# Decoder layer: in the last attention batch, heads turned by groups for all rows, three quarters of the out product taken ahead, LayerNorm roots in pairs

## The chip, the cores and the metric

The kernel runs on one core of one Trainium2 chip. The metric is the device time of one execution in microseconds (us). An execution was profiled once; instruction times below are us from the start of its span. PE is TensorE, PEld its weight loads, DVE is VectorE, ACT ScalarE, POOL GpSimd, SP SyncE, which here only issues DMAs.

## What is computed

```
x = layernorm(x + attention(x, Wq, Wk, Wv, Wo))      # x: (4, 512, 512), 16 heads of 32
x = layernorm(x + experts(x, token ids, ctx))        # 4 experts of 512x512, one per row
x = layernorm(x + ffn(x, w_gate, w_up, w_down))      # 2:4 sparsified hidden layer of 2048
```

Attention: `scores = q k^T`, masked by multiplication with a lower triangle (so masked scores are 0 and still take part), softmax of `scores / sqrt(512)`, times v, heads side by side, times Wo. LayerNorm has no weights: `(x - mean) / sqrt(var + 1e-5)`. In the expert stage each token goes through the expert that its token id chooses, `silu(x W) * (x W)` times W with W from ctx, and is added to x.

## The kernel before

**Stages.** `attention` is one block of instructions for all five engines, `late` (experts and FFN) the next. At the end of a block all engines meet at a barrier and jump; the first instructions of `late` stand behind it. `late` begins with SP loading 128-row tiles of `sorted_dram` (L1424), the DRAM buffer into which attention's rows are scattered in the order of their experts, and with PE turning the first of them (L1513). PE then runs almost without a gap to the end.

**Precision.** Products are made of three: a number is kept as a high part (`_hi`, rounded by an ACT copy) and a low part (`_lo`, the DVE difference), and `matmul3` (L32) issues hi*hi, hi*lo and lo*hi for each of the four slices of 128 of the contraction: 12 matmuls of 128x512 for a 128x512 output tile.

**Attention.** A batch has 512 rows in four row blocks r of 128 and 16 heads in four groups m of 4 heads (128 columns of the concatenated heads). A head has three units u: row blocks (2, 0), then 3, then 1, so a batch has 48 units. For a unit, PE makes scores (L462), DVE their maxima (L764, L775, L778), ACT the exponentials `probs` (L619), PE transposes them (L473), ACT and DVE halve them (`pt_hi` L629, `pt_lo` L784), PE multiplies with v (L489, two units later), and after a head's third unit ACT copies its output out of PSUM (`copy_out`, L654) and POOL adds its parts (L227 to L230). When a group of 4 heads is there, `norm_heads` divides it by the softmax sums into `o_raw`: on POOL for m = 0, 1, 2 (six instructions, about 6.6 us), on DVE for m = 3, where nothing follows it. The order on each engine is written out by hand: `batch(b, more)` in the block of each engine; `more` is false in the last batch (b = 3).

**The end of a batch**, in the order of the list `between`: for each row block r, PE turns all 4 groups of `o_raw` (`turn_heads`, L528: 4 transposes of 128x128 into one bank, one for each group), ACT and DVE halve the turned block (`turned_hi` L663, `turned_lo` L816), PE takes the out product with Wo (`out_product`, 12 matmuls), DVE adds x (`add_x`, L828) and takes mean and variance (`ln.statistics`, L938 and L940), POOL makes 1/sqrt(var + eps) (`ln.rstd`, L969, L973), and the row block is normalized. In the first three batches this is done by ACT with a bias `-mean/sqrt` that POOL makes too (L971, L977; `scale_act` L964), in the last batch by DVE (`ln.scale`, L945). POOL then issues the indirect DMA that scatters the 128 rows (L352). POOL works in order: root of r, then the DMA of r - 1. After the last DMA it waits until all scatters have landed (`pool.wait_ge(s_sc, ...)`) before it goes to the barrier.

In the last batch ACT and DVE also cut the expert weights into high and low parts at the end: `cut_hi` (L1237) for experts 0 to 3 and `cut_lo` (L1241) for experts 0 and 1 before the adds; `cut_lo` for 2 and 3 is DVE's first work in `late`.

## Time and profile before

| | us |
|---|---|
| median of 3 runs | 1136.07 |
| lowest and highest run | 1134.1, 1136.53 |
| the profiled execution | 1132.93 |
| its span (first to last instruction) | 1131.1 |
| PE busy | 1045.4 (92%) |
| DVE busy | 746.5 (66%) |
| ACT busy | 480.6 (42%) |
| POOL busy | 291.2 (26%) |

The attention block takes the first 446 us. Of the page's 40 equal slices of the span, PE is least busy, between 0.4 and 0.5, in the one from 424 to 452. A timeline row reads: start, duration, engine, line and operation, output from inputs, how many merged, and in brackets how long the engine had been idle before it and whose result ended that. `<-issue` means that nothing in the profile explains the wait.

### The profile page before, as it was taken

To read this page: it belongs to the slowest core of one execution; us is meant where nothing else is said; L and a number is where in the kernel's file an instruction comes from. 1 tells how busy PE (TensorE), PEld (TensorE's weight loads), DVE (VectorE), ACT (ScalarE), POOL (GpSimd) and SP (SyncE) were. 2 spreads that over 40 slices of the span, in tenths; PEclk is the share of its full clock that TensorE was granted. 3 is DMA by queue.
4 is the path that set the end of the run, shared out by engine and by line. 5 is a ranking of instruction groups with operands and counts; after the bars stand their busy time and mean duration, and the time that the engine had idled before them with its cause. 6 is when DMAs were issued, how large, how long until landed. Compare 5 with 4: busy or idle time off the path is not lost.

```text
span 1131.1 us, 18084 instructions
## 1 busy us (share of the span) xinstructions
PE 1045.4 (92%) x6022; PEld 845.0 (75%) x6023; DVE 746.5 (66%) x1765; ACT 480.6 (42%) x890; POOL 291.2 (26%) x490
## 2 busy tenths in 40 slices
PE   7889988999998864999999999999999999999994
PEld 6667776767776653788788888888888888888873
DVE  5898699768868886465756655555565545664666
ACT  5787488648846891222324213221232122221113
POOL 2186346544733642123220004100000000000222
PEclk9999999999999987999999999999999999999997
DMA  8877266726743742123533003310020001100101
GB/s 256 239 182 201 65 196 182 202 75 168 200 119 103 190 157 74 38 84 105 193 130 119 23 1 38 38 38 1 1 75 22 16 0 37 37 1 1 38 38 75
DMA packets 55217, 106.19 MB, mean 94 GB/s; under 512 B 6240, under 2 KB 8288, under 8 KB 55136
## 3 DMA queue, kind: packets, MB, share of 16 engines
q1 hardware_dynamic: 50256, 90.99, 29.0%
q0 software_dynamic: 4880, 14.18, 3.4%
q8 instruction: 44, 0.72, 0.3%
q14 instruction: 37, 0.30, 0.1%
HBM read 72.11 MB, written 30.94 MB: 91 GB/s over the span
## 4 chain that ended last, share of the span: by engine, by line
PE 56%; DVE 2%; DMA 1%; ACT 0%; issue 0%; POOLq 0%; POOL 0%; ACTq 0%; SPq 0%; DVEq 0%
PE f_bank L42 54%; PE f_bank L1521 1%; PE f_bank L1513 1%; PE f_bank L1563 1%; DVE rows_kept L1860 0%; DVE ln_stats L938 0%; DMA fw_raw<-gate 0%; DMA rows<-sorted_dram 0%; DVE hs_lo L1848 0%; DVE gu L1764 0%; DVE ln_mv L940 0%; ACT L951 0%; POOLq L1307 0%; DVE h L1838 0%; ACT hs_hi L1690 0%
## 5 line engine op out<-in xcount | busy, mean ns | idle before, releaser
L1667 ACT ACTIVATE fsg<-f_bank 128x512 f32<-128x512 f32 x64 | 38.3, 599 | 298.6 <-PE f_bank L42 298.5
L1799 DVE TENSOR_TENSOR h<-f_bank,fsg 128x512 f32<-128x512 f32 x64 | 44.2, 691 | 181.2 <-PE f_bank L42 181.1
L473 PE MATMUL bank<-ident,probs 128*128 128x128 f32 x640 | 108.8, 285 | 33.8 <-DVE pt_lo L784 22.7
L764 DVE CUSTOM_DVE_ANT_0 bank<-bank,mask 128x384 f32<-128x384 f32 (+3 forms) x256 | 123.1, 503 | 20.2 <-PE bank L462 19.6
L619 ACT ACTIVATE probs<-bank,nmax 128x384 f32<-128x384 f32 (+3 forms) x256 | 129.7, 539 | 15.0 <-DVE nmax L775 13.4
L969 POOL TENSOR_SCALAR ln_var<-ln_mv 128x1 f32<-128x1 f32 x43 | 10.0, 232 | 466.2 <-DVE ln_mv L940 464.9
L784 DVE TENSOR_TENSOR pt_lo<-bank,pt_hi 128x512 f16<-128x512 f32 (+1 forms) x192 | 114.7, 597 | 15.4 <-ACT pt_hi L629 15.0
L629 ACT ACTIVATE pt_hi<-bank 128x512 f16<-128x512 f32 (+1 forms) x192 | 103.0, 536 | 34.1 <-PE bank L473 33.4
L42 PE MATMUL bank<-x_hi,w_qk 128*128 128x512 f32 x256 | 104.3, 416 | 6.8 <-DVE x_lo L789 6.8
L42 PE MATMUL f_bank<-wd_hi,hs_hi 128*128 128x512 f32 x256 | 100.4, 392 | 3.2 <-DVE rows_kept L1860 3.2
L473 PEld LDWEIGHTS bank<-ident,probs 128*128 128x128 f32 x640 | 67.0, 141 | 45.4 <-ACT probs L619 22.4
L42 PE MATMUL f_bank<-wd_hi,hs_lo 128*128 128x512 f32 x256 | 100.4, 392 | 0.0
L42 PE MATMUL f_bank<-wd_lo,hs_hi 128*128 128x512 f32 x256 | 100.1, 391 | 0.0
L42 PE MATMUL f_bank<-big_hi,wg_hi 128*128 128x512 f32 x240 | 93.8, 391 | 0.0
L42 PE MATMUL f_bank<-big_hi,wu_lo 128*128 128x512 f32 x240 | 93.5, 389 | 0.0
L42 PE MATMUL f_bank<-big_hi,wg_lo 128*128 128x512 f32 x240 | 93.4, 389 | 0.0
L42 PE MATMUL f_bank<-big_lo,wg_hi 128*128 128x512 f32 x240 | 93.4, 389 | 0.0
L42 PE MATMUL f_bank<-big_hi,wu_hi 128*128 128x512 f32 x240 | 93.4, 389 | 0.0
L42 PE MATMUL f_bank<-big_lo,wu_hi 128*128 128x512 f32 x240 | 93.4, 389 | 0.0
L462 PE MATMUL bank<-big_lo 128*128 128x384 f32 (+3 forms) x256 | 83.2, 371 | 1.1 <-DMA big_lo<-k_lo_dram 1.1
L489 PEld LDWEIGHTS bank<-v,pt_hi 128*128 128x128 f16 x640 | 49.6, 97 | 39.4 <-issue 29.1
L489 PE MATMUL bank<-v,pt_hi 128*128 128x97 bf16 x640 | 75.0, 211 | 2.3 <-DVE pt_lo L784 2.1
(236 smaller groups left out, 2452.8 us busy)
## 6 DMA issues: line engine op xcount, KB each, us to landing
big_lo<-q_hi_dram SPq DMA_DIRECT2D x32, 256.0 KB, 4.0
big_lo<-q_lo_dram SPq DMA_DIRECT2D x32, 256.0 KB, 4.5
big_lo<-k_hi_dram SPq DMA_DIRECT2D x32, 256.0 KB, 3.9
big_lo<-k_lo_dram SPq DMA_DIRECT2D x32, 256.0 KB, 5.2
rows<-sorted_dram SPq DMA_DIRECT2D x19, 256.0 KB, 2.7
q_hi_dram<-q_hi SPq DMA_DIRECT2D x16, 256.0 KB, 2.4
q_lo_dram<-q_lo SPq DMA_DIRECT2D x16, 256.0 KB, 2.5
k_hi_dram<-k_hi SPq DMA_DIRECT2D x16, 256.0 KB, 3.5
```

The costliest lines, as they stand in the source:

```text
L42: ins = pe.matmul(out, a(k, i), b(k, j), start=(n == 0), stop=(n == len(chain) - 1))
L462: ins = pe.matmul(S[u % SR][:, at:at + cols(r)], stack[0][m % 2][:, h, r * P:(r + 1) * P], stack[1][m % 2][:, h, 0:cols(r)], start=True, s ...
L473: ins = pe.transpose(TP[u % TR][:, j * P:(j + 1) * P], probs[u % RP][:, j * P:(j + 1) * P], ident[:, :])
L489: ins = pe.matmul(out[:, at:ONE + 1], p, v3[:, j, c, at:ONE + 1], start=(n == 0), stop=(n == len(chain) - 1))
L619: ins = act.activation(probs[u % RP][:, at:at + cols(r)], S[u % SR][:, at:at + cols(r)], ACT.Exp, bias=nmax[:, r, c:c + 1])
L629: act.activation(pt_hi[u % RP][:, 0:n], TP[u % TR][:, 0:n], ACT.Copy).then_inc(s_hi, 1)
L764: dve.tensor_tensor_reduce(out=S[u % SR][:, at:at + cols(r)], in0=S[u % SR][:, at:at + cols(r)], in1=mask[:, T - cols(r):T], scale=1.0, sc ...
L784: dve.tensor_tensor(pt_lo[u % RP][:, 0:n], TP[u % TR][:, 0:n], pt_hi[u % RP][:, 0:n], ALU.subtract).then_inc(s_lo, 1)
L1513: ins = pe.transpose(XB[q % 2][:, k * P:(k + 1) * P], rows[q][:, k * P:(k + 1) * P], ident[:, :])
L1521: ins = pe.transpose(EG[i][:, k * P:(k + 1) * P], gu[i][:, k * P:(k + 1) * P], ident[:, :])
L1667: act.activation(fsg[v % 2][:, :], GB[v % 2][:, :], ACT.Silu).then_inc(s_sg, 1)
L1799: dve.tensor_tensor(h[r % 2][:, j, :], UB[v % 2][:, :], fsg[v % 2][:, :], ALU.mult).then_inc(s_h, 1)
```

## The change

The last batch gets its own end; the other three keep `between`.

- PE turns **groups for all rows**: `turn_group(m)` transposes group m of all four row blocks into one bank, behind units 25, 33 and 46 for m = 0, 1, 2 and behind the heads for m = 3. ACT and DVE halve each (`group_hi`, `group_lo`, 128x512) one unit later into slice m of `x_hi` and `x_lo`, which held x turned.
- PE takes the **out product in two parts**: `last_product(r, 0, 9)`, the nine matmuls of groups 0 to 2, at unit 48 for row block 0 (ahead of unit 46 times v), at unit 49 for row block 1 (ahead of unit 47 times v), behind that for 2 and 3; then group 3 is turned and halved and each row block gets its last three matmuls. The four outputs lie in four banks.
- DVE adds and takes statistics for all four row blocks; `cut_lo` of experts 0 and 1 stands behind these. ACT does its four `cut_hi` around `group_hi(3)` and then normalizes all row blocks.
- POOL makes the **roots in pairs** (four instructions on two columns each), then issues two DMAs, twice.
- The wait for the scatters moves from POOL's end of `attention` to SP's first load (and to POOL's start) in `late`, behind the barrier.

```diff
-                for n in range(NB + 1):
-                    if n < NB:
-                        ln.rstd(pool, b * NB + n, n, more)
...
-            pool.wait_ge(s_sc, B * NB * 16)
+                else:
+                    for n in range(0, NB, 2):
+                        ln.rstd(pool, b * NB + n, n, tiles=2)
+                        for r in (n, n + 1):
+                            place(r)
...
+            def turn_group(m):
...
+                for r in range(NB):
+                    ins = pe.transpose(turn_bank(m)[:, r * P:(r + 1) * P],
+                                       o_raw[:, r, m * HPT:(m + 1) * HPT, :].rearrange("p h d -> p (h d)"),
+                                       ident[:, :])
+            def last_product(r, first, last):
+
+                pe.wait_ge(s_otl, LAST * NB + (last + 2) // 3)
+                return matmul3(pe, LB[r][:, :], lambda k, i: x_hl[i][:, k, r * P:(r + 1) * P],
+                               lambda k, i: (wh, wl)[i][3][:, k, :], KT, first, last)
...
+                    if not more and u in part_at:
+                        last_product(part_at[u], 0, 3 * (KT - 1))
                     if u + AHEAD_V >= 0:
                         values(b, u + AHEAD_V)
+                    if not more and u in turn_at:
+                        turn_group(turn_at[u])
+                if not more:
+                    for r in range(len(part_at), NB):
+                        last_product(r, 0, 3 * (KT - 1))
+                    turn_group(NM - 1)
+                    for r in range(NB):
+                        last_product(r, 3 * (KT - 1), 3 * KT).then_inc(s_wo, 1)
...
+                if not more:
+                    group_lo(NM - 1)
+                    for r in range(NB):
+                        add_x(b, r)
+
+                    dve.wait_ge(s_vp, B * NB)
+                    for e in range(len(context.raw) // 2):
+                        context.cut_lo(dve, e)
...
+            sp.wait_ge(s_sc, NT * 16)
             for n in range(3):
                 load(n, n)
```

PE at the end of the last head, before (a last unit times v, then bank by bank the transposes and products; bank4 and bank7 take the out products of row blocks 0 and 1):

```order
L489 MATMUL bank6<-v3,pt_hi3 128x97
L489 MATMUL bank6<-v3,pt_lo3 128x65
L528 MATMUL bank5<-ident,o_raw 128x128 x4
L528 MATMUL bank6<-ident,o_raw 128x128 x4
L42 MATMUL bank4<-big_hi,ot_hi0 128x512 x2
L42 MATMUL bank4<-big_hi,ot_lo0 128x512
```

The same place now (bank0 and bank1 take row blocks 1 and 2):

```order
L42 MATMUL bank0<-big_hi,x_lo 128x512
L505 MATMUL bank6<-v3,pt_hi3 128x97
L505 MATMUL bank6<-v3,pt_lo3 128x65
L505 MATMUL bank6<-v3,pt_hi3 128x97
L505 MATMUL bank6<-v3,pt_lo3 128x65
L42 MATMUL bank1<-big_hi,x_hi 128x512 x2
L42 MATMUL bank1<-big_hi,x_lo 128x512
L42 MATMUL bank1<-big_hi,x_hi 128x512 x2
L42 MATMUL bank1<-big_hi,x_lo 128x512
L42 MATMUL bank1<-big_hi,x_hi 128x512 x2
L42 MATMUL bank1<-big_hi,x_lo 128x512
```

Nine matmuls for row block 1 now stand ahead of the last unit times v, and 18 more between it and the last group's transposes, which were the next thing before.

POOL's last instructions of the attention block, before (`z0` to `z3` are the row blocks):

```order
L969 TENSOR_SCALAR ln1_var<-ln1_mv 128x1
L973 TENSOR_TENSOR ln1_r<-ln1_var,ln1_half 128x1
L352 DMA sorted_dram<-z1,idx_all 2432x512
L969 TENSOR_SCALAR ln1_var<-ln1_mv 128x1
L973 TENSOR_TENSOR ln1_r<-ln1_var,ln1_half 128x1
L352 DMA sorted_dram<-z2,idx_all 2432x512
L352 DMA sorted_dram<-z3,idx_all 2432x512
```

and now:

```order
L357 DMA sorted_dram<-z0,idx_all 2432x512
L357 DMA sorted_dram<-z1,idx_all 2432x512
L1031 TENSOR_SCALAR ln1_var<-ln1_mv 128x2
L1033 TENSOR_SCALAR ln1_minus<-ln1_mv 128x2
L1036 TENSOR_TENSOR ln1_r<-ln1_var,ln1_half 128x2
L1040 TENSOR_TENSOR ln1_moved<-ln1_minus,ln1_r 128x2
L357 DMA sorted_dram<-z2,idx_all 2432x512
L357 DMA sorted_dram<-z3,idx_all 2432x512
```

The second pair's roots moved behind the DMAs of the first pair.

## Rows read from the trace of the kernel before

**Rows 1.** Stretches: start:end, length, busy of PE, PEld, DVE, ACT, POOL, clock, DMA.

```profile
404.00:408.00 4.00, 2.99 (x40) 2.49 (x36) 3.60 (x15) 3.77 (x10) 3.78 (x5) 1.00 0.86 314
...
416.00:428.00 12.00, 8.22 (x29) 6.44 (x29) 9.20 (x14) 8.88 (x7) 0.01 (x1) 0.58 0.00 1
...
437.00:450.00 13.00, 0.12 (x2) 0.05 (x1) 5.87 (x7) 0.00 (x0) 4.83 (x10) 0.69 0.33 116
```

**Rows 2.** The chain of waits that ended last, where the attention block ends.

```profile
446.62 3.29 DMA rows<-sorted_dram
```

**Rows 3.** Timeline of ACT: copies of heads 6 and 7, in batches 2 and 3.

```profile
280.98 0.49 ACT L654 ACTIVATE o_part<-bank 128x388 f32<-128x388 f32 x1
...
285.36 0.56 ACT L654 ACTIVATE o_part<-bank 128x388 f32<-128x388 f32 x1
...
383.46 0.49 ACT L654 ACTIVATE o_part<-bank 128x388 f32<-128x388 f32 x1
...
387.29 0.49 ACT L654 ACTIVATE o_part<-bank 128x388 f32<-128x388 f32 x1
```

**Rows 4.** Timeline of ACT and DVE around the end of the last head.

```profile
414.43 0.51 ACT L654 ACTIVATE o_part<-bank 128x388 f32<-128x388 f32 x1
...
416.27 0.49 ACT L654 ACTIVATE o_part<-bank 128x388 f32<-128x388 f32 x1 [0.77 <-PE bank L489]
...
414.58 0.69 DVE L784 TENSOR_TENSOR pt_lo<-bank,pt_hi 128x512 f16<-128x512 f32 x1 [0.16 <-ACT pt_hi L629]
```

**Rows 5.** Timeline of PE behind the heads.

```profile
419.45 1.94 PE L528 MATMUL bank<-ident,o_raw 128*128 128x128 f32 x8 [3.22 <-DVE o_raw L265]
421.95 1.22 PE L42 MATMUL bank<-big_hi,ot_hi 128*128 128x512 f32 x2 [0.56 <-DVE ot_lo L816]
...
427.24 1.05 PE L528 MATMUL bank<-ident,o_raw 128*128 128x128 f32 x4
...
434.83 0.63 PE L42 MATMUL bank<-big_hi,ot_hi 128*128 128x512 f32 x2
...
435.53 0.62 PE L42 MATMUL bank<-big_hi,ot_hi 128*128 128x512 f32 x2
```

**Rows 6.** Timeline of DVE: first add, what follows its statistics, last add and statistics.

```profile
427.48 0.69 DVE L828 TENSOR_TENSOR z<-bank,x_raw 128x512 f32<-128x512 f32 x1 [0.32 <-PE bank L42]
...
429.14 0.69 DVE L816 TENSOR_TENSOR ot_lo<-bank,ot_hi 128x512 fp32r<-128x512 f32 x1
...
437.11 0.69 DVE L828 TENSOR_TENSOR z<-bank,x_raw 128x512 f32<-128x512 f32 x1 [0.59 <-PE bank L42]
...
438.68 0.18 DVE L940 BATCH_NORM_AGGREGATE ln_mv<-ln_stats 128x2 f32<-128x6 f32 x1
```

**Rows 7.** Timelines of POOL and ACT: roots, normalizing and scatter, batches 3 and 2.

```profile
439.06 0.31 POOL L969 TENSOR_SCALAR ln_var<-ln_mv 128x1 f32<-128x1 f32 x1 [0.55 <-DVE ln_mv L940]
...
441.86 0.96 POOL L352 DMA_INDIRECT sorted_dram<-z,idx_all  x1 [0.31 <-issue]
...
342.24 0.23 POOL L969 TENSOR_SCALAR ln_var<-ln_mv 128x1 f32<-128x1 f32 x1 [4.04 <-DVE ln_mv L940]
...
343.45 0.19 POOL L977 TENSOR_TENSOR ln_moved<-ln_minus,ln_r 128x1 f32<-128x1 f32 x1
...
351.98 0.82 ACT L964 ACTIVATE z<-z,ln_moved,ln_r 128x512 f32<-128x512 f32 x1
...
353.62 0.96 POOL L352 DMA_INDIRECT sorted_dram<-z,idx_all  x1 [0.86 <-ACT z L964]
```

**Rows 8.** The scatter's line: the 16 DMAs' time to landing.

```profile
DMA to landing us min/median/max: 2.7/2.9/6.4
```

**Rows 9.** POOL's scatters in the late block, and DVE's cutting of expert weights.

```profile
577.39 1.07 POOL L1470 DMA_INDIRECT ordered_dram<-y,slot_idx  x1 [1.47 <-DVE y L945]
...
583.86 1.34 POOL L1470 DMA_INDIRECT ordered_dram<-y,slot_idx  x1 [1.47 <-DVE y L945]
...
422.67 4.48 DVE L1241 TENSOR_TENSOR big_hi<-rows_kept,big_lo 128x2048 fp32r<-128x2048 f32 x2
```

More of the change, by code:

```diff
@@ L213, in attention, with turn_bank @@
         rows_at = {1: 2, 3: 3}
+        LAST = B - 1
+        LB = (PJ, S[0], S[1], S[2])
+        turn_at = {25: 0, 33: 1, 46: 2}
+        part_at = {UPB: 0, UPB + 1: 1}
+        def turn_bank(m):
+            return PJ if m < NM - 1 else TP[0]
         wo_at = {5 + 2 * k: k for k in range(KT)}
@@ L564, in batch @@
                         project(b, *pieces[u])
+                    if not more and u in part_at:
+                        last_product(part_at[u], 0, 3 * (KT - 1))
                     if u + AHEAD_V >= 0:
                         values(b, u + AHEAD_V)
-                for step, r in between:
-                    if step == "v" and more:
+                    if not more and u in turn_at:
[6 more added lines that the diff above has]
+                        last_product(r, 3 * (KT - 1), 3 * KT).then_inc(s_wo, 1)
+                for step, r in between if more else ():
+                    if step == "v":
                         v_product(r)
@@ L574, in batch @@
                         out_product(b, r)
-                    elif step == "scores" and more:
+                    elif step == "scores":
                         pe.wait_ge(s_vr, (b + 2) * NB)
@@ L579, in batch @@
                             scores(b + 1, u)
-                    elif step == "sum" and more:
+                    elif step == "sum":
                         v_sum(b + 1, r)
@@ L700, in batch @@
                         copy_out(b, u // UPH - 1)
+                    if not more and u - 1 in turn_at:
+                        group_hi(turn_at[u - 1])
                 above(b, NM - 1)
@@ L709, in batch @@
                         context.cut_hi(act, e)
-                for step, r in between:
-                    if step == "v" and more:
+                    group_hi(NM - 1)
+                    for e in range(2, len(context.raw)):
+                        context.cut_hi(act, e)
+                    for r in range(NB):
+                        norm_rows(b, r)
+                for step, r in between if more else ():
+                    if step == "v":
                         v_split(b + 1, (r, r + 1))
@@ L714, in batch @@
                         turned_hi(b, r)
-                        if not more and r == 1:
-                            for e in range(2, len(context.raw)):
-                                context.cut_hi(act, e)
-                    elif step == "scores" and more:
+                    elif step == "scores":
                         for u in range(AHEAD_S):
                             exps(b + 1, u)
-                    elif step == "out" and more and r >= 2:
+                    elif step == "out" and r >= 2:
                         norm_rows(b, r - 2)
@@ L852, in batch @@
                             v_above(0, n)
+                    if not more and u - 1 in turn_at:
+                        group_lo(turn_at[u - 1])
                 norm_heads(dve, 1, b, NM - 1)
-                for step, r in between:
-                    if step == "v" and more:
+                if not more:
+                    group_lo(NM - 1)
+                    for r in range(NB):
+                        add_x(b, r)
+                    dve.wait_ge(s_vp, B * NB)
+                    for e in range(len(context.raw) // 2):
+                        context.cut_lo(dve, e)
+                for step, r in between if more else ():
+                    if step == "v":
                         v_split(b + 1, (r, r + 1))
@@ L858, in batch @@
                         turned_lo(b, r)
-                        if not more and r == 1:
-                            dve.wait_ge(s_vp, B * NB)
-                            for e in range(len(context.raw) // 2):
-                                context.cut_lo(dve, e)
                     elif step == "out":
                         add_x(b, r)
-                        if r >= 1 and not more:
-                            norm_rows(b, r - 1)
-                    elif step == "scores" and more:
+                    elif step == "scores":
                         for u in range(AHEAD_S):
@@ L873, in batch @@
                         negated(b + 1, AHEAD_S - 1)
-                    elif step == "sum" and more:
+                    elif step == "sum":
                         v_above(b + 1, r)
-                if not more:
-                    norm_rows(b, NB - 1)
             def qk_lo(i):
@@ L1482, in _ @@
             for n in range(NS):
-                ln2.rstd(pool, n, n % 4)
+                ln2.rstd(pool, n, n % 4, False)
                 place(n)
```

72 lines of the change are left out of this document (48 added, 24 removed).

## Prediction

> **What bounds the kernel now.** I read the stretches first, then the timelines between us 404 and 450. In the heads all engines are close to full: of 4 us ACT works 3.77 and DVE 3.60, PE only 2.99 [rows 1]; a step added there for ACT or DVE is not free. Behind the heads PE waits 3.22 us for the last group's normalizing, then starts its transposes at 419.45, and between 416 and 428 has a mean clock of 0.58, most of it the lower level, 1.2 GHz [rows 1, 5]. From 421.95 to 427.24 it makes 12 matmuls, 0.44 us each; near 435 three take 0.70 us, 0.23 each [rows 5]. From 437 to 450 PE does nothing: the chain runs through DVE and POOL (adds, roots, scatters), the barrier, and the first load, issued at 446.62 and landed 3.29 us later [rows 1, 2]. Behind that load PE is full to the end, so the issue time of this load is what the change can move: each us there is a us of the kernel. The last scatter begins at 441.86, 4.76 us earlier [rows 7]. So the sum is: where does the last scatter begin now, and how long from it to the load.
>
> **1. Group turns in the heads.** Groups 0 and 1 add, at two places, 4 transposes on PE, one ACT copy and one DVE difference of 128x512 (0.69, as L784 in [rows 4]). PE has a quarter of its time idle; ACT and DVE have not. The nearest rows: in batch 2 the stretch from one head's copy to the next holds two more ACT copies (halving x) and takes 4.38 us (280.98 to 285.36), the same stretch of batch 3 without them 3.83 (383.46 to 387.29) [rows 3]: 0.28 for each. Here DVE's part comes on top, and for group 1 ACT also waits for PE's transposes. Bounds: 0.1 each, if the slack takes them, and 1.1 each, if both parts lie on the path. I take **+1.0** for both. POOL's norms of the groups end before the turns, so they add no wait.
>
> **2. Group 2 and the first partial products.** Group 2's turn stands behind unit 46's transposes; ACT halves it behind the copy of head 14, which starts at 414.43 [rows 4] and holds ACT 0.5, so to about 415.5; DVE's difference ends at 416.2. PE waits for it at unit 48, about 1 us, and then makes nine matmuls (2.1 us at 0.233), unit 46 times v (0.3), nine more (2.1), unit 47 times v. The copy of head 15, at 416.27 before [rows 4], starts at about 421.2: +4.9. Its copy and normalizing take 3.2 us as before (416.27 to 419.45) [rows 4, 5], to 424.4; PE meanwhile makes 18 matmuls (4.2 us) and is done at 425.25, so PE ends last, not DVE. The 3.22 us wait is gone.
>
> **3. The last group and the last quarter.** Transposes 0.6, ACT 0.6, DVE 0.7, three matmuls 0.9: the first add starts at 428.1. Before it was at 427.48 [rows 6]: **+0.7**, and with part 1 +1.7, so 429.1. The nine twelfths taken ahead save less than they cost here, because they stand ahead of the last head's own output. ACT's cut_hi still fit ahead of and behind the last group.
>
> **4. Adds.** From an add to the next instruction behind its statistics DVE takes 1.66 us (427.48 to 429.14), from the last add to the end of its variance 1.75 (437.11 to 438.86) [rows 6]. PE brings a row block every 0.7 us, so DVE sets the pace: first add to last variance 3*1.66 + 1.75 = 6.7 us instead of 11.4. **-4.7**: this is the gain of the change.
>
> **5. Roots and scatters.** Before, the last variance leads to the last scatter in 441.86 - 438.86 = 3.0 us [rows 6, 7]. Now count from the second variance, at 1.66 + 1.75 = 3.4 us behind the first add. POOL starts 0.2 later [rows 7]. The four root instructions take 1.4 us for one column (342.24 to 343.64); two columns and the slower 0.31 of L969 in batch 3 make it 1.66. ACT's normalizing takes 0.82, and the scatter that waits for it starts 0.82 after it ends (352.80 to 353.62) [rows 7]. A scatter lasts 0.96 to 1.1 and the next comes 0.31 later [rows 7], or lasts 1.34 beside DVE's cutting of weights [rows 9]: 1.4 between two, 1.07 for the second. Then the same again for the pair 2 and 3, whose variances are long there: POOL is the bound. 3.4 + 0.2 + 2*(1.66 + 0.82 + 0.82 + 1.4) + 1.07 + 0.2 = 14.3 us from first add to last scatter, plus 0.5 for scatters beside cut_lo, which now runs there: 14.8. Before it was 441.86 - 427.48 = 14.4. So the gain of part 4 is given back whole: **+5.1**, and parts 4 and 5 together are +0.4. The first pair costs two waits for ACT that DVE's scaling hid before.
>
> **6. The barrier.** Before: scatter at 441.86, landed 2.7 us later [rows 8] at 444.56, load issued at 446.62: 2.06 for POOL's waking, barrier and jump. Now POOL goes to the barrier when its last scatter's 0.96 is over, while it flies; barrier end is 0.96 + 0.2 + 1.9 = 3.06 behind its start, by when it has landed, and SP's new wait costs nothing. 3.06 instead of 4.76: **-1.7**. Bounds: 0, if the jump waits for something else than the engines, and -2.06. Queued behind SP's wait are only the loads that need it; DVE's two cut_lo (4.5 us) start with the barrier's end as before, and still end before ACT's first copy of the turned rows.
>
> **Sum.** +1.0 + 0.7 - 4.7 + 5.1 - 1.7 = **+0.4 us**; I say +0.5. The profiled execution had a span of 1131.1 and 1132.93 in all, 3.1 below the median 1136.07; the difference is carried over to the median: **1136.6 us**. A change of 0.2%, 2.3 us, is about what a measurement of this kernel can tell.
>
> **Rivals.**
>
> *A, a faster one: the heads take the turns into their slack, and POOL's and ACT's hand-overs are shorter.* The 0.82 from a finished ACT to the scatter is issue time; if it runs beside the root or beside the previous scatter, as in the two scatters 0.31 apart [rows 7], 2*0.5 is saved; +1.0 in the heads becomes +0.2; the clock level behind the barrier comes back up to a us sooner. -0.8 - 1.0 - 1 against +0.5: -2.3 and beyond, 1133.5. Against it: three scatters that waited for ACT all started that late.
>
> *B, DVE and POOL on one path to memory.* cut_lo, two instructions of 2.24 us each [rows 9], stood ahead of the adds, where POOL was idle; it now starts at the last variance, 6.7 us behind the first add, and ends 4.5 later, at 11.2. The second pair's roots start at 3.4 + 0.2 + 1.66 + 1.64 + 1.4 + 1.07 + 0.2 = 9.6. If POOL's small instructions must wait for the one that runs, they start at 11.2: +1.6, so +2.1 in all, 1138.2. Rows speak for little: beside four differences of 128x512 with both inputs in SBUF a scatter lasted 1.34 instead of 1.07 [rows 9]; but that is a scatter, and none shows a root in that place. The Trainium skill (SBUF — State Buffer, Who interferes with whom) says that a VectorE instruction with two SBUF inputs and a GpSimd instruction that reads SBUF exclude each other for the whole instruction, whoever is first. By that rule B is what happens.
>
> *C, slower: the clock.* PE stopped behind the heads and the granted clock was at the lower level for the transposes and the next 12 matmuls [rows 5]. In the new order PE stands about 1 us ahead of the nine matmuls of unit 48. If the clock falls there, the 36 matmuls ahead of the last group run at up to 0.43: 0.2 more each, 7 us, or, if it returns after the 7.8 us that it took before (419.45 to 427.24), 7.8/2 = 3.9; all of it is on the path. +0.5 + 3.5: 1140. It decides only if the stop at unit 48 is as long as the one before, 3.2 us; 1 us speaks against it.
>
> *D*: the wait in SP's queue or the jump keeps the whole 4.76: +2.2, 1138.3.
>
> **Chances.** Forecast 0.42, by itself 1135 to 1138.3. A 0.22, B 0.20, C 0.08, D 0.08. Range 1132.5 to 1140. Faster by over 0.2% (below 1133.8): A, 0.22. Slower by over 0.2% (above 1138.3): C, half of B and D, and the upper edge of the forecast: 0.25. Within: 0.53.
>
> **What would show it.** First add about 1.7 us later than 427.48, last variance near 436, last scatter near 443.9, first load near 447. Part 1: head copies behind us 387 later by 0.3 to 0.6 at units 26 and 34. Part 2: the copy of head 15 at about 422, PE busy without a gap over 1.5 us from there. B: POOL's first root of the second pair begins when a cut_lo ends. C: 0.4 us a matmul in the partial products. Wrong if the last scatter starts before 441 or the load is not 3 us behind it.

## The result

The changed kernel takes **1138.23 us** (median of 13 runs, 1136.32 to 1139.96); the kernel before took 1135.38 in the same series (13 runs, 1132.71 to 1136.53). The ratio is 1.0029, 95% interval 1.0020 to 1.0038: 0.29% slower. A second series, shown below, gave 1.0016 (1.0004 to 1.0028). The forecast was 1136.6 and "within 0.2%": the time lies inside the range, 1.6 us above the forecast. In us it stays just below the slow bound of 1138.3; as a ratio it is beyond 0.2% in this series and not in the second. It is rival B's number, 1138.2, and nearly rival B's mechanism, but the number is in part luck: B had +2.1 on 1136.07, and it was +2.85 on 1135.38.

### The profile after

The profiled execution has a span of 1136.0 us, 4.9 more than before. 1.70 of that arise ahead of everything that was changed: the copy of head 7 in batch 3 starts at 388.99, not at 387.29 [rows 3]. I therefore compare distances from that copy on, and from one landmark to the next.

ACT, timeline: the copies of heads 14 and 15 out of PSUM (answers to [rows 4]), and the two pairs of row blocks that it normalizes.

```profile
416.80 0.51 ACT L703 ACTIVATE o_part<-bank 128x388 f32<-128x388 f32 x1
423.61 0.50 ACT L703 ACTIVATE o_part<-bank 128x388 f32<-128x388 f32 x1 [5.44 <-PE bank L505]
...
435.96 1.52 ACT L1023 ACTIVATE z<-z,ln_moved,ln_r 128x512 f32<-128x512 f32 x2 [3.44 <-POOL ln_moved L1040]
444.48 1.52 ACT L1023 ACTIVATE z<-z,ln_moved,ln_r 128x512 f32<-128x512 f32 x2 [7.00 <-POOL ln_moved L1040]
```

PE, timeline: start of the partial products, the turn of the last group, and the last quarter (answers to [rows 5]).

```profile
418.57 0.73 PE L42 MATMUL bank<-big_hi,x_hi 128*128 128x512 f32 x2 [0.93 <-DVE x_lo L879]
...
427.69 0.60 PE L573 MATMUL bank<-ident,o_raw 128*128 128x128 f32 x4
429.70 0.73 PE L42 MATMUL bank<-big_hi,x_hi 128*128 128x512 f32 x2 [1.41 <-DVE x_lo L879]
```

DVE, timeline: first add, last variance, `cut_lo` (answers to [rows 6]).

```profile
430.70 0.69 DVE L890 TENSOR_TENSOR z<-bank,x_raw 128x512 f32<-128x512 f32 x1 [1.05 <-PE bank L42]
...
437.35 0.18 DVE L999 BATCH_NORM_AGGREGATE ln_mv<-ln_stats 128x2 f32<-128x6 f32 x1
437.45 4.49 DVE L1304 TENSOR_TENSOR big_hi<-rows_kept,big_lo 128x2048 fp32r<-128x2048 f32 x2
```

POOL, timeline: roots of a pair and two scatters, twice (answers to [rows 7]), and SP's first loads behind the barrier (to [rows 2]).

```profile
434.34 0.24 POOL L1031 TENSOR_SCALAR ln_var<-ln_mv 128x2 f32<-128x2 f32 x1 [15.95 <-DVE ln_mv L999]
...
437.60 3.12 POOL L357 DMA_INDIRECT sorted_dram<-z,idx_all  x1 [1.67 <-ACT z L1023]
441.03 1.76 POOL L357 DMA_INDIRECT sorted_dram<-z,idx_all  x1 [0.30 <-issue]
442.86 0.23 POOL L1031 TENSOR_SCALAR ln_var<-ln_mv 128x2 f32<-128x2 f32 x1
...
446.11 1.07 POOL L357 DMA_INDIRECT sorted_dram<-z,idx_all  x1 [1.67 <-ACT z L1023]
447.49 0.96 POOL L357 DMA_INDIRECT sorted_dram<-z,idx_all  x1 [0.31 <-issue]
...
451.56 0.13 POOL L992 MEMSET ln_half<- 128x1 f32 x2 [3.11 <-POOLq L69]
```

```profile
451.25 2.60 SPq L1487 DMA_DIRECT2D rows<-sorted_dram  x4
```

PE, timeline: the first turn of sorted rows in `late` and the fifth, before and after. By the fifth turn PE is back in its rhythm of one turn in about 6.45 us, so that is where I stop counting.

```profile
449.95 1.11 PE L1513 MATMUL f_bank<-ident,rows 128*128 128x128 f32 x4 [12.88 <-DMA rows<-sorted_dram]
...
475.61 0.60 PE L1513 MATMUL f_bank<-ident,rows 128*128 128x128 f32 x4
```

```profile
454.37 1.12 PE L1578 MATMUL f_bank<-ident,rows 128*128 128x128 f32 x4 [21.62 <-DMA rows<-sorted_dram]
...
480.48 0.60 PE L1578 MATMUL f_bank<-ident,rows 128*128 128x128 f32 x4
```

What to see: the first two scatter rows are the surprise. A scatter took 0.96 to 1.34 us in every row of before; here two take 3.12 and 1.76, and both begin inside DVE's `cut_lo` (437.45 to 441.94). The sum, step by step:

| from ... to | before | after | difference | predicted |
|---|---|---|---|---|
| copy of head 7 to copy of head 14 | 27.14 | 27.81 | +0.67 | +1.0 |
| to the first add | 13.05 | 13.90 | +0.85 | +0.7 |
| to the end of the last variance | 11.38 | 6.83 | -4.55 | -4.7 |
| to the last scatter | 3.00 | 9.96 | +6.96 | +5.1 |
| to the first load | 4.76 | 3.76 | -1.00 | -1.7 |
| to PE's first turn | 3.33 | 3.12 | -0.21 | 0 |
| to PE's fifth turn | 25.66 | 26.11 | +0.45 | 0 |
| sum | 88.32 | 91.49 | **+3.17** | +0.4 |

The 3.17 us agree with the 2.85 between the medians. But the column "before" is one execution, and a long one behind the heads: in e3 and h1 below, in which nothing is changed up to the last product, the first add came 12.64 us behind the copy of head 14 (13.05 here) and the last variance 10.54 and 10.78 behind the first add (11.38 here). In this profile the third row block's transposes still ran at the lower clock (1.05 us, [rows 5]; 0.60 in h1). Against those two the changed kernel's gain from the adds would be 3.7 to 4.0 and not 4.55.

### The profile page after: what moved, and what is told of

It reads as the page before. It is cut to its first block, busy times and chain, and to the rows that moved or that the text cites. A ratio compares the mean times of both kernels' runs of the same rounds, so it can differ in the third digit from the quotient of the medians.

```text
span 1136.0 us, 18082 instructions
## 1 busy us (share of the span) xinstructions
PE 1043.8 (92%) x6022; PEld 843.0 (74%) x6023; DVE 743.7 (65%) x1761; ACT 482.6 (42%) x894; POOL 293.9 (26%) x490
## 4 chain that ended last, share of the span: by engine, by line
PE 56%; DVE 2%; DMA 1%; ACT 0%; issue 0%; POOLq 0%; POOL 0%; ACTq 0%; SPq 0%; DVEq 0%
PE f_bank L42 54%; PE f_bank L1586 1%; PE f_bank L1578 1%; PE f_bank L1628 1%; DVE rows_kept L1925 0%; DVE ln_stats L997 0%; DMA fw_raw<-gate 0%; DMA rows<-sorted_dram 0%; DVE hs_lo L1913 0%; DVE gu L1829 0%; DVE ln_mv L999 0%; ACT L1010 0%; POOLq L1370 0%; DVE h L1903 0%; ACT hs_hi L1755 0%
## 5 line engine op out<-in xcount | busy, mean ns | idle before, releaser
L1031 POOL TENSOR_SCALAR ln_var<-ln_mv 128x1 f32<-128x1 f32 (+1 forms) x41 | 9.3, 228 | 463.5 <-DVE ln_mv L999 462.1
L489 PEld LDWEIGHTS bank<-ident,probs 128*128 128x128 f32 x640 | 67.5, 141 | 45.1 <-ACT probs L668 22.5
```

Of the source, the lines that this page charges most:

```text
L489: ins = pe.transpose(TP[u % TR][:, j * P:(j + 1) * P], probs[u % RP][:, j * P:(j + 1) * P], ident[:, :])
```

## The experiments

Theory P: `cut_lo` beside the scatters is what makes the change slow, by holding the scatters. Its rival O: the order of pairs itself (two waits for ACT, 1.67 us of idle each) is the price, and not the scatters' length. Every ratio below is to the kernel before on the same chip. Chips differ: the median of before was between 1133.75 and 1136.16 in the five series.

### cut_lo early: `e1_cut_early`

```diff
+                if not more:
+                    dve.wait_ge(s_vp, B * NB)
+                    for e in range(len(context.raw) // 2):
+                        context.cut_lo(dve, e)
                 norm_heads(dve, 1, b, NM - 1)
...
                     for r in range(NB):
                         add_x(b, r)
-
-                    dve.wait_ge(s_vp, B * NB)
-                    for e in range(len(context.raw) // 2):
-                        context.cut_lo(dve, e)
```

ACT's first two `cut_hi` move ahead of the copy of head 15 too.

> The change with one thing moved: the first two cut_hi of ACT and the two cut_lo of DVE stand in the wait for the last head's output instead of at the last group and behind the adds. Theory P (DVE's cut_lo, which reads two SBUF inputs, holds POOL up while it issues the scatters): with DVE free the first scatter takes 1.1 us instead of 3.12 and the second 0.96 to 1.1 instead of 1.76, so the second pair's roots start 2.7 us sooner, and from first add to last scatter it takes 14.1 us instead of 16.8; the time is 2.5 to 3 us under the change's, level with the kernel before. Rival Q (the first scatter is long for a reason of its own, it is the first work of POOL after a long idle stretch and its rows come from ACT): 3.1 and 1.8 us stay, and 16.8 us too. Both: PE's partial products are not later, since DVE has 4.7 us and ACT 5.4 us idle there.

Measured: 1133.13 us, ratio 0.9995 (0.9981 to 1.0009). POOL's timeline:

```profile
435.16 1.10 POOL L357 DMA_INDIRECT sorted_dram<-z,idx_all  x1 [1.67 <-ACT z L1023]
436.57 0.96 POOL L357 DMA_INDIRECT sorted_dram<-z,idx_all  x1 [0.30 <-issue]
437.60 0.23 POOL L1031 TENSOR_SCALAR ln_var<-ln_mv 128x2 f32<-128x2 f32 x1
```

The first pair's scatters take 2.06 us together, not 4.88, and from first add to last scatter it is 13.95 us in place of 16.79: the 2.84 are the scatters' 2.82. The copy of head 15 is as far behind that of head 14 as in the changed kernel (6.83 and 6.81), and the first add 0.21 later behind it (14.11 and 13.90), so `cut_lo` and `cut_hi` cost little in their new place. P holds, and within what these runs can tell (0.14% either way) its price is the whole loss against before.

### Single roots: `e2_single_roots` and `e4_early_single`

```diff
-                    for n in range(0, NB, 2):
-                        ln.rstd(pool, b * NB + n, n, tiles=2)
-                        for r in (n, n + 1):
-                            place(r)
+                    for n in range(NB + 1):
+                        if n < NB:
+                            ln.rstd(pool, b * NB + n, n, False)
+                        if n > 0:
+                            place(n - 1)
...
                         add_x(b, r)
+                        if r > 0:
+                            ln.scale(dve, z[r - 1], z[r - 1], b * NB + r - 1, r - 1, s_x1)
+                    ln.scale(dve, z[NB - 1], z[NB - 1], b * NB + NB - 1, NB - 1, s_x1)
```

This is the root, scaling and scatter order of the kernel before, behind the new adds; ACT no longer normalizes. e2 leaves `cut_lo` late, e4 moves it as e1 does.

> The change with the pairs undone: POOL makes one root at a time and scatters the row block before, as in the kernel before, and DVE normalizes; cut_lo stays behind DVE's last work. If the pairs with ACT's normalizing cost what the prediction said, two hand-overs from ACT of 0.82 + 0.82 us each and four root instructions instead of two, and the cutting the rest, then first add to last scatter falls from 16.8 us to 12 to 12.5 us: DVE takes 2.2 us for each row block with its scaling, last scaling near 9.5 us behind the first add, scatters about 2.6 us apart, and only the last one beside cut_lo. The time is then about 4 us under the change's, 1 us under the kernel before. Rival: POOL's issue of scatters alone is the bound (4 times 1.4 us behind each other): then single roots gain under 1 us.

> Both of the first two edits on the change: cut_lo early and single roots with DVE's scaling. If the two costs add up: first add to last scatter 12 us instead of 16.8 (14.4 in the kernel before), last scatter near 442.5 instead of 447.5 on the change's scale, and the time 4.5 to 5 us under the change's, 1.5 to 2 us under the kernel before. If cutting and pairs are one cost counted twice, it is no faster than the better of the two.

Measured: e2 1134.27 us, ratio 1.0002 (0.9991 to 1.0014); e4 1132.08 us, ratio 0.9981 (0.9972 to 0.9991), faster than both kernels. From first add to last scatter both take 10.89 us, less than the 12 to 12.5 expected (pairs with early `cut_lo`: 13.95). So the pairs have a price of their own beside P's, 3.06 us in the profiles. In the time e4 leads e1 by 0.14%, 1.6 us, with intervals that overlap; in the profiles 0.50 of the 3.06 go to the load's landing and 1.50 to the distance from first to fifth turn, 28.24 and 26.74. In e2 only the last scatter meets `cut_lo`. DVE and POOL there:

```profile
439.23 0.55 DVE L1006 TENSOR_SCALAR z<-z,ln_mv,ln_r 128x512 f32<-128x512 f32 x1 [0.77 <-POOL ln_r L1038]
439.69 4.49 DVE L1306 TENSOR_TENSOR big_hi<-rows_kept,big_lo 128x2048 fp32r<-128x2048 f32 x2
```

```profile
439.39 1.34 POOL L357 DMA_INDIRECT sorted_dram<-z,idx_all  x1 [0.19 <-issue]
441.03 1.78 POOL L357 DMA_INDIRECT sorted_dram<-z,idx_all  x1 [0.30 <-issue]
```

But e2's first load comes 4.58 us behind the last scatter, not 3.76: now the barrier waits for DVE, whose `cut_lo` ends at 444.17. With that, and with 28.18 from first to fifth turn, e2 missed its forecast in the time: it was to be 1 us under the kernel before and is level with it.

### What holds a scatter: `f3_cut_in_eight`

In the changed kernel `cut_lo` is two instructions of 2.24 us, so the first ends at 439.69 and the second at 441.94. The first scatter ends at 440.72, the second at 442.79: 1.03 and 0.85 behind an end. e2's last one ends at 442.81, 0.88 behind 441.93. It looks as if a scatter were held until the one running instruction is over. The 1.34 fits too. In e2 above the scatter of 439.39 ends at 440.73, 0.95 behind the end of DVE's scaling (439.23 to 439.78), which reads one block out of SBUF and not two. The kernel before has the same two rows, and beside its scatter of [rows 9] (583.86 to 585.20) this difference, which ends at 584.25, again 0.95 ahead:

```profile
440.06 0.55 DVE L945 TENSOR_SCALAR z<-z,ln_mv,ln_r 128x512 f32<-128x512 f32 x1 [0.77 <-POOL ln_r L973]
440.22 1.34 POOL L352 DMA_INDIRECT sorted_dram<-z,idx_all  x1 [0.19 <-issue]
...
583.57 0.68 DVE L1276 TENSOR_TENSOR wu_lo<-fw_raw,wu_hi 128x512 fp32r<-128x512 f32 x1
```

So the hold could be read from the kernel before: each 1.34 is about 0.95 us of its own and 0.39 left of the instruction in whose midst it began. No experiment here changes the scaling, so for that one the hold is read and not tested.

```diff
-                        context.cut_lo(dve, e)
+                        dve.wait_ge(context.s_hi, e + 1)
+                        for k in range(KT):
+                            ins = dve.tensor_tensor(context.lo[:, e, k], context.raw[e][:, k],
+                                                    context.hi[:, e, k].bitcast(F32), ALU.subtract)
+                        ins.then_inc(context.s_lo, 1)
```

> Edit: the changed kernel, and DVE's two late cut_lo of 128x2048 are made as eight of 128x512, about 0.6 us each, 4.6 in all, in the same place. Theory H (a scatter issued while such an instruction runs is held until that one instruction ends, then takes its own 0.9 to 1.0): in the changed kernel the first scatter, 437.60 to 440.72, ends 1.03 behind the end of the first cut_lo (439.69), the second, 441.03 to 442.79, ends 0.86 behind the end of the second (441.93). With eight short ones the scatters should last 1.3 to 1.6, the second pair's roots come about 1.7 us sooner, and the whole goes down by 1.7: ratio to the kernel before 1.0014. Rival S (DVE takes a share of the path as long as it works at all): scatters of 3.1 and 1.8 again and 1.0029. Rival of both: DVE is slowed instead, and the eight last over 5 us.

Measured: 1139.41 us, ratio 1.0032 (1.0018 to 1.0047). DVE, then POOL:

```profile
436.94 4.90 DVE L923 TENSOR_TENSOR big_hi<-rows_kept,big_lo 128x512 fp32r<-128x512 f32 x8
```

```profile
437.09 1.52 POOL L357 DMA_INDIRECT sorted_dram<-z,idx_all  x1 [1.67 <-ACT z L1027]
438.92 1.36 POOL L357 DMA_INDIRECT sorted_dram<-z,idx_all  x1 [0.31 <-issue]
440.34 0.39 POOL L1035 TENSOR_SCALAR ln_var<-ln_mv 128x2 f32<-128x2 f32 x1
440.81 0.52 POOL L1037 TENSOR_SCALAR ln_minus<-ln_mv 128x2 f32<-128x2 f32 x1
441.30 1.13 POOL L1040 TENSOR_TENSOR ln_r<-ln_var,ln_half 128x2 f32<-128x2 f32 x1
```

As theory H says: 1.52 and 1.36 in place of 3.12 and 1.76, with DVE just as busy over the same stretch. What remains is partly moved: the second pair's roots now run beside the pieces too, and take 0.39, 0.52 and 1.13 where alone they take 0.23, 0.23 and 0.72, so small POOL instructions are held as well. From first add to last scatter it is 15.65 us, 1.14 less than in the changed kernel. The time did not follow (1.0014 was expected): the fifth turn comes 27.99 us behind the first, not 26.11. That distance is the second thing that the prediction's sum lacked.

### The barrier alone: `e3_barrier_only`

```diff
-            pool.wait_ge(s_sc, B * NB * 16)
...
+            sp.wait_ge(s_sc, NT * 16)
             for n in range(3):
                 load(n, n)
```

> The kernel before with only the wait for the scatters moved from POOL's end of the first block to SP's first load in the next. Prediction: the load comes 3.1 us behind the last scatter's start instead of 4.8, -1.7 us. The trace of the change shows 3.8 us, which is -1.0. Theory: the barrier takes as long whether POOL comes from a semaphore or from its scatter, so 3.8 and -1.0 here as well. Rival: in the change the way from last scatter to load is stretched by something of its own (the pair behind each other), and here it is 3.1.

Measured: 1134.11 us, ratio 0.9999 (0.9990 to 1.0009). The last scatter leads to the load in 3.75 us, as in the changed kernel and in e1 and e4, against 4.76: -1.0 is the edit's worth, and it is there. But the load now takes 4.04 to PE's first turn (3.33 before), and the fifth turn comes 28.21 behind the first (25.66). PE's stretches of 4 us in this kernel; the last columns are granted clock (1.00 is 2.4 GHz, 0.50 is 1.2), DMA share and GB/s:

```profile
450.00:454.00 4.00, 3.24 (x8) 2.57 (x9) 0.62 (x1) 1.20 (x1) 0.00 (x0) 0.50 0.00 0
454.00:458.00 4.00, 3.02 (x14) 2.23 (x12) 1.20 (x2) 1.09 (x2) 0.00 (x0) 0.77 0.00 0
458.00:462.00 4.00, 3.23 (x10) 2.40 (x9) 0.78 (x2) 0.60 (x1) 0.00 (x0) 0.66 0.00 0
```

and in the kernel before:

```profile
450.00:454.00 4.00, 2.50 (x7) 1.83 (x8) 1.86 (x2) 1.88 (x2) 0.00 (x0) 0.50 0.23 82
454.00:458.00 4.00, 3.37 (x14) 2.53 (x12) 0.40 (x1) 1.03 (x2) 0.00 (x0) 0.82 0.00 0
458.00:462.00 4.00, 2.87 (x14) 2.25 (x15) 1.58 (x3) 0.66 (x2) 0.00 (x0) 1.00 0.00 0
```

In both PE starts `late` at the lower level, having stood for over 12 us. Before, the clock comes back once; in e3 it comes back and falls again at about 459 for 3.5 us, and matmuls at the lower level start 0.43 us apart, not 0.23. That second fall is in the profiles of e2, e3, e4, f3 and g2, and in these alone the distance from first to fifth turn is 28.0 to 28.2; in the six others where PE stands still it is 25.7 to 26.9, and grows there with the time that the clock takes to come back: 5.5 us behind the first turn before, 8.7 in f2. Most of these kernels have one profile, and one profile need not be typical of its kernel: f2 below is e4 but for a wait in SP, has no second fall, and takes the same time. On e3 itself the interval holds both the 1 us expected and none, so what the runs show is that no gain above 1.1 us arrived.

### Why the first load lands late: `f2_first_load_alone`

```diff
             for n in range(3):
                 load(n, n)
+                if n == 0:
+                    sp.wait_ge(s_rows[0], 16)
```

on e4's kernel.

> Edit: the kernel of e4_early_single, and SP waits until the first load of sorted rows has landed before it issues the next ones. Theory L (the first four loads share the 16 DMA engines): load issue to PE's first turn was 3.0 to 3.1 where the four issues took 2.53 to 2.60 us, 3.33 where they took 2.19, 3.49 to 4.04 where they took 1.77. Alone the first should be there 2.5 to 2.8 behind its issue: first turn about 0.8 us earlier than e4's 445.16. The second turn comes 7.8 behind the first and its rows have landed by then. Rival: the time to landing is the first load's own and varies by itself: 3.5 again. In the total theory L gives -0.8 at most, and less if the clock at the lower level takes it back; 1131.3 to 1132.

Measured: 1134.12 us, ratio 0.9983 (0.9971 to 0.9996), the same as e4. From the load's issue to PE's first turn it is 3.56 us with the load alone on the queues, against e4's 3.53. Theory L falls. Why this step takes 3.03 (e1), 3.12 and 3.22 (the changed kernel, twice), 3.33 (before), 3.45 to 3.66 (most) and 4.04 (e3) stays open.

### Partial products behind the heads: `f4_part_behind`

```diff
-        part_at = {UPB: 0, UPB + 1: 1}
+        part_at = {}
```

> Edit: the changed kernel with none of the partial products between the last units; all 36 matmuls of the first three quarters stand behind the last unit times v. Copy of head 15 about 4.3 us earlier than in the changed kernel. If PE ends last (the term of part 2 of the prediction), the first add moves by -0.6 to 0 only: ratio 1.0025 to 1.003. If the copy and normalizing of head 15 set the first add, it moves by -1.5 to -4 and the ratio is below 1.002. A third: PE stands for 0.9 us or longer while cut_hi and the copy wait, and nothing is gained since ACT's cut_hi (4 us) take ACT's place ahead of the last group.

Measured: 1138.38 us, ratio 1.0019 (1.0003 to 1.0036), not told from the changed kernel. The copy of head 15 comes 2.46 us behind that of head 14, in place of 6.81, and the first add 13.75 behind it, in place of 13.90. So delaying the last head's output by 4.35 us costs 0.15: PE's 36 matmuls fill that time in either order. This bears out part 2.

### Turns out of the heads: `g2_turns_late`

```diff
-        turn_at = {25: 0, 33: 1, 46: 2}
+        turn_at = {44: 0, 45: 1, 46: 2}
```

> Edit: the changed kernel, and groups 0 and 1 are turned and halved behind units 44 and 45, next to group 2, and not in the heads. Part 1 of the prediction: from the copy of head 7 to that of head 14 the changed kernel took 416.80 - 388.99 = 27.81, the kernel before 414.43 - 387.29 = 27.14. Without turns in the heads it should be 27.1 to 27.2 again. What the two turns cost at the end instead: two ACT copies and two DVE differences, 0.6 to 0.7 each, on engines that are as full there as in the heads, 0.3 to 1.2 us on the copy of head 15 or ahead of the nine matmuls. First add behind the copy of head 7: 41.71 in the changed kernel; 41.4 to 42.3 here. Ratio 1.002 to 1.004: no gain from moving them. Rival: the turns in the heads cost more than their 0.67 (they also shift ACT against PE), and the first add comes over 0.7 sooner.

Measured: 1141.12 us, ratio 1.0049 (1.0031 to 1.0067). ACT, timeline: the copies of heads 7, 13 and 14.

```profile
388.33 0.49 ACT L703 ACTIVATE o_part<-bank 128x388 f32<-128x388 f32 x1
...
411.72 0.49 ACT L703 ACTIVATE o_part<-bank 128x388 f32<-128x388 f32 x1
416.97 0.51 ACT L703 ACTIVATE o_part<-bank 128x388 f32<-128x388 f32 x1
```

From head 7 to head 13 it is 23.39 us; in the second profile of the changed kernel, below, 24.06. That is the 0.67 again. Side by side at the end the two turns cost 1.9: the first add is 42.99 behind the copy of head 7, against 41.74. The places in the heads are the cheap ones. This was more than expected: units 44 and 45 stand ahead of the copy of head 14, which came 28.64 behind that of head 7 and not 27.1 to 27.2, and 1.0049 is above the 1.002 to 1.004.

### The changed kernel once more: `g4_changed_again`

> The changed kernel itself, on the same chip as the two others and with a second profiled execution. If the reading of its trace holds, the scatters of the first pair last 3.1 and 1.8 us again, from last scatter to load 3.76, ratio 1.002 to 1.004. What is open is the distance from PE's first turn to its fifth in the late block: 26.1 in the first profile. If it comes out at 27 or 28 here, this distance changes from one execution to the next by 2 us and can't be put down to an edit; if it is 26.1 again, it goes with the kernel.

Measured: 1137.34 us, ratio 1.0016 (1.0004 to 1.0028). POOL's first pair:

```profile
437.21 3.13 POOL L357 DMA_INDIRECT sorted_dram<-z,idx_all  x1 [1.67 <-ACT z L1023]
440.64 1.75 POOL L357 DMA_INDIRECT sorted_dram<-z,idx_all  x1 [0.30 <-issue]
```

The held scatters return to within 0.01 us; the copies of heads 7 and 14 are 27.81 apart again, and first and fifth turn 25.77 (26.11). So the distance to the fifth turn moved by 0.34 between two executions of the same kernel, not by 2.

### Keeping PE busy: `f1_pe_busy`, `g1_pe_busy_longer`, `h1_before_pe_busy`

Theory K: the lower clock at the start of `late` costs 3 us or more in every one of these kernels, because PE stands still ahead of it. Test: give PE work that nobody reads, behind the last products and ahead of the first turn. g1's edit, on e4's kernel (f1 has 36 and 12 in place of 44 and 18; h1 is the kernel before with 33 and 18):

```diff
                         last_product(r, 3 * (KT - 1), 3 * KT).then_inc(s_wo, 1)
+                    for _ in range(44):
+                        pe.matmul(TP[0][:, :], x_hl[0][:, 0, 0:P], wh[3][:, 0, :], start=True, stop=True)
...
+            for i in range(18):
+                pe.transpose(YB[3][:, 0:P], ident[:, :], ident[:, :])
             x_transposes(0, 0)
```

> Edit: the kernel of e4_early_single, and PE is kept busy through the wait: 36 matmuls of 128x512 into a bank that nobody reads behind the last products (about 8.4 us, from about 429 to 437.5), and 12 transposes of the identity ahead of the first turn of the late block. They compute nothing of the output. Theory K (clock): in e4 the first turn stands at 445.16 and the fifth at 473.40, 28.24 later; in the kernel before these are 449.95 and 475.61, 25.66. The 2.6 us more are matmuls at the lower level, granted clock 0.50 from 434 to 450 and 0.63, 0.80, 0.78 up to 462. With PE busy the clock should stand at 1.00 at the first turn, and the fifth come about 22.5 later (four periods of 6.45 less the two short ones at the start): -3 to -5 us, 1127 to 1129. Rival (no clock term; the distance is set by DMA and DVE): first turn 445.2 and 28.2 to the fifth as before, the same time as e4, about 1132. Third: the extra work delays the barrier or the first turn, and it is 1 us slower.

> Edit: the kernel of f1_pe_busy with 44 matmuls behind the last products in place of 36, one behind the other into a bank that nobody reads, and 18 transposes of the identity in place of 12 ahead of the first turn. In f1 PE stopped at 441.5, the barrier ended at 445.7, and the granted clock was 0.86 between 442 and 446 and 0.50 from there to the first turn, so the clock had not been held. Here PE should stop at about 443, 2 us less ahead of the barrier's end, and start again at once. Theory K (the clock at the first turn is what the 25.7 to 28.2 us from the first to the fifth turn hang on): clock 1.00 at the first turn, the 12 matmuls of the first products at 0.23 and not 0.43, fifth turn about 22.5 to 23.5 behind the first, and 2 to 3 us less than e4: ratio about 0.995 to 0.996. If the clock falls all the same, the distance is 25.7 again and the ratio 0.998. Rival (PE's 44 matmuls hold the barrier, or the 18 transposes at the lower level end behind the landing): first turn 0.5 to 1.2 later, ratio 0.998 to 0.999 even with the clock held.

> Edit: the kernel before, and PE kept busy through its wait by work that nobody reads: 33 matmuls of 128x512 behind the last product (436.9 to about 444.6) and 18 transposes of the identity ahead of the first turn of the late block. Theory K: the clock is as much a cost of the kernel before as of the changed one. PE's distance from first to fifth turn 25.66 becomes about 24.5 (24.49 in g1_pe_busy_longer), the first turn stays near 449.95 or moves by up to +0.3: -1.0 to -1.2 us, ratio 0.9990 to 0.9992. Then g1's lead of 0.44% is for the larger part the order of adds, roots and scatters with an early cut_lo, with a clock that would else have taken part of it back. Rival: the busy PE alone gives as much as in g1 against e4 (2.5 us or more), ratio 0.998 or less, which would mean that the distance of 25.66 in the one profile of before was a lucky one.

Measured:

| kernel | us | ratio (interval) | PE still ahead of `late` | first to fifth turn |
|---|---|---|---|---|
| e4 | 1132.08 | 0.9981 (0.9972 to 0.9991) | 16.12 | 28.24 |
| f1 | 1132.82 | 0.9978 (0.9965 to 0.9990) | 4.25 | 25.76 |
| g1 | 1130.81 | 0.9956 (0.9943 to 0.9969) | 2.40 | 24.49 |
| h1 | 1132.38 | 0.9972 (0.9960 to 0.9983) | 1.90 | 24.38 |

(The stillness of e4 runs to the first turn, that of the others to the transposes behind the barrier.) PE's timeline in g1:

```profile
446.05 3.00 PE L1685 MATMUL f_bank<-ident 128*128 128x128 f32 x18 [2.40 <-PEq L69]
449.49 1.12 PE L1582 MATMUL f_bank<-ident,rows 128*128 128x128 f32 x4 [0.44 <-DMA rows<-sorted_dram]
452.11 0.50 PE L42 MATMUL f_bank<-big_lo,xt_hi 128*128 x1 [1.50 <-DVE xt_lo L1814]
452.45 0.39 PE L42 MATMUL f_bank<-big_hi,xt_hi 128*128 x1
452.68 0.40 PE L42 MATMUL f_bank<-big_lo,xt_lo 128*128 x1
```

and stretches of 1 us, the same columns as those of e3 and before above:

```profile
446.00:447.00 1.00, 0.95 (x9) 0.98 (x10) 0.95 (x1) 0.00 (x0) 0.33 (x4) 1.00 0.09 6
447.00:448.00 1.00, 1.00 (x9) 1.00 (x7) 1.00 (x1) 0.00 (x0) 0.00 (x0) 0.60 0.87 217
...
450.00:451.00 1.00, 0.61 (x3) 0.21 (x1) 0.54 (x1) 0.35 (x1) 0.00 (x0) 0.70 0.41 154
451.00:452.00 1.00, 0.00 (x0) 0.00 (x0) 0.69 (x1) 0.98 (x2) 0.00 (x0) 1.00 0.00 0
```

The clock is still up when the barrier ends, is down from 447.2 to 450.6 (my reading of the 0.60 and the 0.70), and is back before the first products, which start 0.23 us apart where e3's start 0.43 apart. So theory K was right on the products but not on the first turn, which still ran at the lower level, and the fifth came 24.49 behind it and not the 22.5 to 23.5 expected. The fifth turn comes 3.75 us sooner behind the first than in e4, and the time is 0.25% lower, about 2.8 us. g1 is the fastest kernel of this study, **0.44% faster** than the kernel before. f1 is a miss: its clock was at the lower level from 444.9 to 455.1, as in a kernel without the extra work. Its profile is 2.5 us shorter than e4's in this distance, its runs show 0.03% against e4, within the intervals.

h1 answers what was foreseen as the rival there: the busy PE alone gives the kernel before 0.28%, 3.2 us, and not the 1.0 to 1.2 that its profile's 25.66 allows. In the profiles h1's distance is 1.28 shorter and its first turn 0.88 nearer to the copy of head 14 (34.64 against 35.52). Those 0.88 are not the extra work's: they arise ahead of it (from the copy of head 14 to the last add h1 takes 21.68, before 22.68, and e3, without extra work, 21.44). That leaves the 1.28, and the interval, 1.9 to 4.5 us, doesn't reach so low; it may be that the one profile of before shows a recovery in `late` better than its usual one. No second profile of before was taken, so this stays open. g1 against h1, both with a busy PE, is what the other parts of the change may be worth once `cut_lo` is early and the roots single: 0.16%, or 1.8 us. The two were measured on different chips and their intervals overlap, so this last figure is not clear of noise.

## Why the forecast was off, step by step

- **What bounds the kernel** ("each us there is a us of the kernel"): the issue of the first load moved by +2.93 us, less the 1.70 taken out, and the medians by 2.85, so for this pair it held. As a rule it isn't safe: in e3 the load came a us sooner behind the last scatter and no gain was seen; in its profile the landing and the clock took 0.7 and 2.55. PE behind the load is full, but not at one speed.
- **Part 1** +1.0: +0.67, shown twice, and by g2 from the other side. Right in mechanism, 0.33 too dear.
- **Parts 2 and 3** +0.7: +0.85. The copy of head 15 was foreseen 4.9 later behind that of head 14 and came 4.97 later; f4 shows that PE and not DVE ends that stretch. Right in mechanism; against e3 and h1 the +0.85 would be +1.26.
- **Part 4** -4.7: -4.55. Right; DVE sets the pace. But 0.60 to 0.84 of it belong to the one profile of before, which was that much longer here than h1 and e3.
- **Part 5** +5.1: **+6.96. This is the step that failed**, by the one term of 0.5 "for scatters beside cut_lo". The nearest row was the 1.34 of a scatter beside four differences of 128x512 [rows 9], with instructions of 0.6 us; these are of 2.24. That 1.34 was itself 0.39 of hold. The scatters took 2.82 more than without them. The rest of the working was 0.35 too dear: without the 0.5 it gave 14.3 from first add to last scatter, and e1 took 13.95.
- **Part 6** -1.7: -1.0, and 3.75 to 3.77 in every kernel with the edit but e2. I had 1.9 us from POOL's arrival to the load; it is 2.8 (447.49 + 0.96 to 451.25). The 2.06 that it came from began at the landing of 2.7 us, which is the shortest of sixteen (the median is 2.9, [rows 8]), and so was no measurement of the barrier. The load 3.76 behind the last scatter, and not 3, is one of the signs of being wrong that the prediction named.
- **Rival B** gave 1138.2 and named the path between DVE and POOL, but put the hold on the second pair's roots and the scatters at 1.4 at most. In the trace those roots start when the scatter before them is issued, 0.92 behind the end of `cut_lo`; the hold fell on both scatters ahead. The Trainium skill (SBUF — State Buffer, Who interferes with whom) has the two exclude each other for the whole instruction, whoever is first. For the issue of a DMA by GpSimd the same section of the Trainium skill infers that a `tensor_tensor` does not hold it; by the scatters' ends and f3's lengths it does, and the measurement decides. DVE lost nothing to it: its two instructions took 4.49 beside scatters (4.48 without, [rows 9]), and 4.50 in f1, where POOL was idle; the second of them began in the midst of a scatter.
- **Rival A** fell: from the end of a pair's roots to its first scatter it is 1.67 us each time, in e1 and the changed kernel alike, where the forecast had 1.64.
- **Rival C** did not come where I put it. PE stood 0.93 ahead of the partial products and 1.41 ahead of the last quarter, and the last group's four transposes took 0.60 where they took 1.05 at the lower level [rows 5]. The lower level came in `late`, where the prediction's sum had no term.
- **Rival D** fell: 3.76, not 4.76.

The range: the terms of the clock and of the landing, which had no row in the sum, added +0.24 here, and up to +3.3 in e3. That they were small in this pair is luck and no merit of the sum.

## What to carry to other kernels

Don't move a long two-input VectorE instruction off an idle stretch to one in which GpSimd issues scatters: do it earlier; splitting it shortened the scatters here, though not the time. Here the move alone made a neutral change slow. Judge a step of GpSimd by the longest single instruction that may run beside it, not by the share of time in which VectorE is busy. And where a barrier or a chain of small steps leaves TensorE still ahead of its long run, price the clock behind it, and try filling the gap with matmuls that nobody reads: on the kernel before this alone gave 0.28%.

## What was not expected of the hardware

- An indirect DMA's issue on GpSimd, 0.96 to 1.1 us alone, took 3.12 and 3.13, 1.75 to 1.78 beside VectorE differences of 128x2048 with both inputs in SBUF (2.24 us each), and 1.36 to 1.52 beside those of 128x512. One begun 0.16 us into a scaling of 128x512 (0.55 us, one block read) took 1.34. Each ended 0.85 to 1.03 us behind the end of the instruction that ran when it began. VectorE's own time didn't change.
- With the wait moved, it was 2.8 to 3.1 us from the end of POOL's last scatter to SP's load and POOL's own first instruction behind the barrier, with all other engines already there.
- After a wait of PE of over 12 us the granted clock came back 5.5 to 8.7 us behind PE's first turn, and in five of eleven profiles fell once more, for 3 to 4 us, before it stayed. Where PE had been busy until 2.4 us or less ahead of the barrier's end (g1, h1) it fell for 3 to 4 us only, and was back before the first products. What decides between one fall and two isn't settled.
